# A new order for the first block of an attention and expert kernel

## The reference

```
def attention(x, y):                      # x: layernormed tokens, y: context
    q = (x @ Wq + bq).reshape(B, N, 16, 32)
    k = (y @ Wk + bk).reshape(B, M, 16, 32)
    v = (y @ Wv + bv).reshape(B, M, 16, 32)
    scores = einsum('bnhd,bmhd->bhnm', q, k) / sqrt(32)
    out = einsum('bhnm,bmhd->bnhd', softmax(scores), v).reshape(B, N, 512)
    return relu(out @ W1 + b1) @ W2 + b2
x = x + attention(layernorm(x), ctx)
top1 = argmax(x2n @ Wg.T)                 # one of 8 experts for each token
x = x + expert[top1](layernorm(x))        # 512 -> 128 (gelu) -> 512
```

## Time and profile before

| | us |
|---|---|
| median of 3 runs | 1470.18 (1470.04 to 1471.04) |
| the profiled execution | 1474.38 |
| its span, first to last instruction | 1472.6 |
| busy: PE, DVE, ACT, POOL | 1446.5, 1038.0, 756.6, 416.6 |
| granted clock of PE, mean of the span | 0.997 |

### The profile page before, as it was taken

The page is one execution under the profiler, slowest core; times in us unless marked ns, Lnnn a source line. Parts: engine busy times, 40 slices in busy tenths (PEclk is TensorE's granted clock), DMA queues, the critical chain, the costliest instruction groups (busy, mean ns, idle before and its releaser), DMA issues.

```text
span 1472.6 us, 23484 instructions
## 1 busy us (share of the span) xinstructions
PE 1446.5 (98%) x7710; PEld 1207.2 (82%) x7710; DVE 1038.0 (70%) x2524; ACT 756.6 (51%) x2097; POOL 416.6 (28%) x306
## 2 busy tenths in 40 slices
PE   7899999999999999999999999999999999999997
PEld 5688787878888888878787888888787878788996
DVE  5767667686868686776868686858676675748666
ACT  4656354544536353645455353635354544547875
POOL 1342221203122222222130312222222212108885
PEclk9999999999999999999999999999999999999999
DMA  7130201203030302131120301130202002357984
GB/s 284 45 102 1 87 1 44 66 27 105 22 100 1 108 15 94 38 84 47 43 81 22 101 13 67 43 90 1 86 1 66 22 29 87 140 176 249 300 262 147
DMA packets 70284, 121.50 MB, mean 83 GB/s; under 512 B 21847, under 2 KB 30304, under 8 KB 69142
## 3 DMA queue, kind: packets, MB, share of 16 engines
q1 hardware_dynamic: 59366, 86.30, 19.2%
q0 software_dynamic: 10800, 33.70, 6.0%
HBM read 75.09 MB, written 46.40 MB: 82 GB/s over the span
## 4 chain that ended last, share of the span: by engine, by line
PE 95%; DVE 3%; ACT 1%; issue 1%; DMA 0%; POOL 0%; POOLq 0%; SPq 0%; DVEq 0%; ACTq 0%
PE bank L1185 24%; PE bank L1207 24%; PE bank L1000 12%; PE bank L1137 8%; PE bank L1026 7%; PE bank L1607 4%; PE bank L1101 4%; PE bank L1645 3%; PE bank L1282 2%; PE bank L1591 2%; PE bank L968 2%; PE bank L1260 1%; DVE actH L1118 1%; ACT actH L1112 1%; PE bank L859 1%
## 5 line engine op out<-in xcount | busy, mean ns | idle before, releaser
L1207 PE MATMUL bank<-w,actH 128*128 128x512 f32 x1536 | 372.1, 393 | 0.0
L1185 PE MATMUL bank<-actA,w 128*128 128x512 f32 x1536 | 370.3, 394 | 0.0
L1185 PEld LDWEIGHTS bank<-actA,w 128*128 128x128 f32 x1536 | 284.2, 188 | 60.9
L1207 PEld LDWEIGHTS bank<-w,actH 128*128 128x128 f32 x1536 | 283.0, 188 | 55.9
L1095 POOL TENSOR_TENSOR E<-E,rc 128x1232 f32<-128x1232 f32 x64 | 144.2, 2254 | 461.3 <-DVE rc L1089 461.3
L1357 POOL DMA_INDIRECT region<-rows,pos x64 | 63.8, 997 | 456.4 <-DVE pos L1351 418.0
L1192 ACT ACTIVATE actH<-bank,b 128x512 fp32r<-128x512 f32 x128 | 88.5, 691 | 187.7 <-PE bank L1185 187.7
L1000 PE MATMUL bank<-actA,wq 128*128 128x512 f32 x768 | 182.4, 390 | 1.7 <-DVE actA L980 1.7
L1068 ACT ACTIVATE E<-bank,mx 128x77 f32<-128x77 f32 x512 | 157.7, 362 | 37.1 <-DVE mx L1035 37.1
L1000 PEld LDWEIGHTS bank<-actA,wq 128*128 128x128 f32 x768 | 144.1, 188 | 32.5 <-issue 2.7
L1014 DVE SCALAR_TENSOR_TENSOR actQ<-bank,bq,actQ 128x512 fp32r<-128x512 f32 x64 | 48.1, 751 | 167.9 <-ACT actQ L1009 167.9
(11 more groups left out here) (172 smaller groups left out, 2121.2 us busy)
## 6 DMA issues: line engine op xcount, KB each, us to landing
rowB<-region SPq DMA_DIRECT2D x71, 258.0 KB
xn<-in_x SPq DMA_DIRECT2D x64, 256.0 KB, 2.9
rows<-in_x SPq DMA_DIRECT2D x64, 256.0 KB, 3.4
w_raw<-in_W SPq DMA_DIRECT2D x2, 2048.0 KB, 11.8
e_raw<-in_E SPq DMA_DIRECT2D x16, 256.0 KB, 3.1
region<-padrow SPq DMA_DIRECT2D x9, 258.0 KB, 2.4
e_parts<-e_high SPq DMA_DIRECT2D x8, 256.0 KB, 2.0
e_parts<-e_low SPq DMA_DIRECT2D x8, 256.0 KB, 2.3
```

The costliest lines, as they stand in the source:

```text
L1185: mm = pe.matmul(p[:], w, a, start=k == 0 and j == 0, stop=k == KD - 1 and j == 2)
L1207: mm = pe.matmul(p[:], a, w, start=m == 0 and j == 0, stop=m == MF - 1 and j == 2)
```

## The change

The beginning of the program is put into another order, and the values are made in three pieces instead of four. The four batches' context rows are 4 x 77 = 308; before, each batch's 77 rows were a product (VP) of their own, now the 308 rows are cut into 128, 128 and 52. The steps that change place:

- KLO 0 and 1 (low parts of keys) stand behind the four XT, with KLO 2 and 3.
- W2's load is a step of its own behind the store of the keys.
- VP 0 stands ahead of the first queries, VP 1 between the scores of groups 1 and 2, VP 2 behind the scores of group 3; before, 2 and 3 stood among the probabilities' transposes and the first values products.
- The low part of a group of queries is a step of its own, QLO, no longer part of Q. In block 0 it stands further behind; in the later blocks directly behind its Q.
- The fourth queries and their QLO move among the scores of groups 0 and 1.
- MASKS moves ahead of the first queries, two W1 conversions move between the first three queries, and SUM of group 3 moves ahead of the first transposes.

```diff
+VR = [min(P, NB * M - i) for i in range(0, NB * M, P)]
+NV = len(VR)
...
-    v_parts = nc.dram_tensor("v_parts", [NB, M, 2, D], F32).ap()
+    v_parts = nc.dram_tensor("v_parts", [NB * M, 2, D], F32).ap()
...
             for c in range(NC):
                 step("PT", b, 0, c)
-            step("SUM", b, KD - 1)
+            if b:
+                step("SUM", b, KD - 1)
             for c in CA:
                 step("PT", b, 1, c)
             if b:
                 step("TT", b - 1, 0)
-            else:
-                step("VP", 2)
             step("AV", b, 0, "C")
             step("COPY", b, 0)
             step("AV", b, 0, "A")
             step("AV", b, 0, "B")
             if b:
                 step("TT", b - 1, 1)
-            else:
-                step("VP", 3)
...
-            if b == 0:
-                step("CONV_W1", 1)
...
         step("KP", 2)
-        step("KLO", 0)
-        step("KLO", 1)
         for s in range(SUB):
             step("XT", 0, s)
         step("KP", 3)
-        step("KLO", 2)
-        step("KLO", 3)
+        for m in range(KD):
+            step("KLO", m)
         step("KSTORE")
+        step("W2_LOAD")
         step("CONV_WQ", 1)
+        step("VP", 0)
         step("KCOPY")
+        step("MASKS")
+        step("VF", 0)
         step("Q", 0, 0)
-        step("Q", 0, 1)
-        step("VP", 0)
-        step("VF", 0)
+        step("QLO", 0, 0)
         step("VHI", 0)
-        step("Q", 0, 2)
         step("VLO", 0)
         step("VLOAD", 0, 0)
         step("VLOAD", 0, 1)
-        step("MASKS")
-        for g in range(KD):
-            for s in range(SUB):
-                step("S", 0, g, s)
-            if g == 0:
-                step("Q", 0, 3)
-            if g == 1:
-                step("VP", 1)
-            if g == 2:
-                step("VF", 1)
-            step("EXP", 0, g)
-            if g:
-                step("SUM", 0, g - 1)
-        step("VHI", 1)
+        step("VSTORE", 0)
         step("CONV_W1", 0)
-        step("VLO", 1)
-        step("VSTORE", 1)
+        step("Q", 0, 1)
+        step("QLO", 0, 1)
+        step("CONV_W1", 1)
+        step("Q", 0, 2)
+        for s in range(SUB - 1):
+            step("S", 0, 0, s)
+        step("QLO", 0, 2)
+        step("Q", 0, 3)
+        step("S", 0, 0, SUB - 1)
+        for s in range(SUB):
+            step("S", 0, 1, s)
+        step("QLO", 0, 3)
+        step("EXP", 0, 1)
+        step("SUM", 0, 0)
+        step("VP", 1)
+        for s in range(SUB):
+            step("S", 0, 2, s)
+        step("SUM", 0, 1)
+        for s in range(SUB):
+            step("S", 0, 3, s)
+        step("EXP", 0, 3)
+        step("VP", 2)
+        step("VF", 1)
+        step("SUM", 0, 2)
+        step("VF", 2)
+        step("SUM", 0, 3)
         step("XLOAD", 0)
...
-                mm = pe.matmul(p[0:M, :], ctxT[:, k, M * i:M * i + M], wv_raw[:, k, :],
+                mm = pe.matmul(p[0:VR[i], :], ctxT[:, k, P * i:P * i + VR[i]], wv_raw[:, k, :],
```

More of the change, by code:

```diff
@@ L166, in xattn_moe_kernel @@
     ctxT = staged("ctxT", [P, KT, NB * M])
-    v_f = [staged(f"v_f{i}", [M, D]) for i in range(2)]
-    bvbc = staged("bvbc", [M, D])
+    v_f = [staged(f"v_f{i}", [P, D]) for i in range(2)]
+    bvbc = staged("bvbc", [P, D])
     assert o[0] <= w2_at + size([P, MF, D], F32)
@@ L176, in xattn_moe_kernel @@
     w2_raw = at("w2_raw", [P, MF, D], F32, w2_at + 4 * MF * D)
[L177 to L180, removed]
+    assert NV == 3 and VR[0] >= M
+    v_hl = [at(f"v_hl{i}", [P, 2, D], F32R, (rows_at[1], xn_at)[i // 2] + i % 2 * size([P, 2, D], F32))
+            for i in range(NV)]
+    assert 2 * size([P, 2, D], F32) <= min(size([P, SUB, ROW], F32), SUB * size([P, D], F32))
     e1 = at("e1", [P, KD, NE, EH], F32, wq_at)
@@ L319, in attention_tail @@
             else:
-                for i in (2, 3):
-                    step("VF", i)
+                for i in (1, 2):
                     step("VHI", i)
-                for i in (2, 3):
+                for i in (1, 2):
                     step("VLO", i)
@@ L488, in xattn_moe_kernel @@
                 step("Y", b, 1)
-                step("Q", b + 1, 0)
-                step("Q", b + 1, 1)
+                for m in range(2):
+                    step("Q", b + 1, m)
+                    step("QLO", b + 1, m)
                 if prep is not None:
@@ L505, in xattn_moe_kernel @@
                         step("Q", b + 1, g + 2)
+                        step("QLO", b + 1, g + 2)
                 if b + 2 == NBLK:
@@ L607, in xattn_moe_kernel @@
         chains = []
-        DRIP = {"Q": 2, "PT": 2, "Y": 1, "TTOUT": 1}
+        DRIP = {"QLO": 2, "PT": 2, "Y": 1, "TTOUT": 1}
         def drip(n):
@@ L665, in sp_xnload @@
                 if b == 1:
-                    sp.wait_ge(st_v, 16 * (NB - 1))
+                    sp.wait_ge(st_v, 16 * NV)
                 if PREP0 + 2 <= b < PREP0 + 2 + NE:
@@ L702, in sp_vload @@
             else:
-                sp.wait_ge(st_v, 16 * (NB - 1))
+                sp.wait_ge(st_v, 16 * NV)
                 sp.wait_ge(S["pe_av"], 3 * NP * BPB * i)
             for c, r, k, m, h in PIECES[len(PIECES) // 2 * part:len(PIECES) // 2 * (part + 1)]:
-                src = v_parts[i, k:k + m] if i else f32(v_hl[0][k:k + m, :, :])
+                src = v_parts[M * i + k:M * i + k + m] if i else f32(v_hl[0][k:k + m, :, :])
                 src = src.rearrange("k s (g x) -> k (s g) x", g=NP)[:, :, HD * h:HD * h + HD]
@@ L716, in sp_vstore @@
             sp.wait_ge(S["dve_v"], i + 1)
-            sp.dma_start(v_parts[i], f32(v_hl[i][:])).then_inc(st_v, 16)
+            k = 0 if i else M
+            sp.dma_start(v_parts[P * i + k:P * i + VR[i]], f32(v_hl[i][k:VR[i]])).then_inc(st_v, 16)
         def sp_e1raw(sp, e):
@@ L866, in dve_vf @@
                 dve.wait_ge(S["pe_xT"], SUB)
-            dve.tensor_tensor(v_f[i % 2][:], of("VP", i)[0:M, :], bvbc[:], ALU.add).then_inc(S["dve_vf"], 1)
+            r = slice(0, VR[i])
+            dve.tensor_tensor(v_f[i % 2][r], of("VP", i)[r, :], bvbc[r], ALU.add).then_inc(S["dve_vf"], 1)
         def act_vhi(act, i):
             act.wait_ge(S["dve_vf"], i + 1)
-            act.activation(v_hl[i][:, 0], v_f[i % 2][:], ACT.Identity).then_inc(S["act_v"], 1)
+            r = slice(0, VR[i])
+            act.activation(v_hl[i][r, 0], v_f[i % 2][r], ACT.Identity).then_inc(S["act_v"], 1)
         def dve_vlo(dve, i):
             dve.wait_ge(S["act_v"], i + 1)
-            dve.tensor_tensor(v_hl[i][:, 1], v_f[i % 2][:], f32(v_hl[i][:, 0]),
+            r = slice(0, VR[i])
+            dve.tensor_tensor(v_hl[i][r, 1], v_f[i % 2][r], f32(v_hl[i][r, 0]),
                               ALU.subtract).then_inc(S["dve_v"], 1)
@@ L915, in pool_zero_row @@
         def pool_zero_row(pool):
-            pool.wait_ge(st_v, 16 * (NB - 1))
+            pool.wait_ge(st_v, 16 * NV)
             pool.wait_ge(ld_v, 16 * VLOADS)
@@ L1709, in xattn_moe_kernel @@
             "KSTORE": {"sp": sp_kstore},
+            "W2_LOAD": {"sp": sp_w2load},
             "CONV_WQ": {"act": act_conv_wq, "dve": dve_conv_wq},
@@ L1725, in xattn_moe_kernel @@
             "XNLOAD": {"sp": sp_xnload},
-            "Q": {"pe": pe_q, "act": act_q, "dve": dve_q},
+            "Q": {"pe": pe_q, "act": act_q},
+            "QLO": {"dve": dve_q},
             "S": {"pe": pe_s, "dve": dve_s, "act": act_s},
```

7 lines of the change are left out of this document (4 added, 3 removed).

## The result

The changed kernel takes 1460.69 us (median of four, 1460.08 to 1462.33) against 1470.61 us for the kernel before (four, 1470.04 to 1472.41). The ratio is 0.9932, with a 95% interval of 0.9915 to 0.9949: faster by 0.5 to 0.85%. The prediction was 1460.3 us in a range of 1456.8 to 1466.0. The profiled execution took 1462.33 us with a span of 1460.5, so the two profiled executions differ by 12.1 us while the medians differ by 9.9.

What follows compares the result with a forecast made beforehand. PE, busy 98%, bounds the kernel; time comes from its waits or work before H. One values product less (2.58), the gap (1.7) and remaining waiting and half-clock time make 9.9 off 1470.18: 1460.3 us, range 1456.8 to 1466.0.

Steps and rivals of the forecast that it cites:

- The walk: Step-by-step timing from the last key product to the first H product: H at 58.55 instead of 68.44 us, 9.9 gained.
- Rival B: PE's clock falls near 49 us, ahead of the values products, for about 6.8: gain 7.0, 1463.2 us; chance 30%.
- "Before, that low part, a values step and the masks held the first maximum", 3.8 gained: First softmax: third queries' low part queued behind three maxima, so exponentials start at 29.85 instead of 33.64 us, 3.8 gained.
- The fourth queries: Group 0's softmax: their copy on ACT, until 34.15 us, now ahead of tile 3's exponentials instead of behind; no separate gain given.
- VP(0) in the gap: First values product placed in PE's gap between last key product and first queries, 18.05 to 19.77 us: 1.7 us.
- One VP less: Values made on PE in three products instead of four: 2.58 us saved.
- SUM of group 3 ahead of the low parts: End of first softmax on DVE: group 3's sums at 45.8 to 47.2 us, low parts from 47.4; no price for the order.
- "Any difference behind H": Sign that the prediction is wrong: any difference after the first H product, where all engines' instructions read alike; no size.
- No stall for loads: First values product runs at 18.05 us without waiting for Wv, first products of values don't wait for gathers; loads cost nothing.

Runs made afterwards that it cites:

- before_fourth_queries: Kernel before with only the fourth queries ahead of group 0's last tile, their low part behind group 1's maxima: 1468.85 us, ratio 0.9984.
- values_behind_q1: Changed kernel with the first values product and its steps back behind the second queries: 1463.80 us, ratio 0.9954 to the kernel before.
- low_part_ahead: Changed kernel with the low part of the third queries back ahead of the first maxima: 1461.91 us, ratio 0.9940 to the kernel before.
- changed_again: Changed kernel run once more, unchanged, in a later group of runs: 1466.76 us, ratio 0.9935 to the kernel before.
- before_third_low_part: Kernel before with only the low part of the third queries moved behind the first three maxima: 1469.74 us, ratio 0.9987.
- the third group of runs: Runs of the changed kernel unchanged and two variants with the first softmax's end reordered; the kernel before took 1475.09 us there instead of 1470.61.

## Why the prediction was right, and where it was not

- **The walk.** It put H 42.22 us behind the last key product; the two profiles at the full clock, each one part away from the change, have 42.25 and 42.26, and after has 43.90 with its low clock. The intermediate stations agree within 0.1 us, counted from the key product: the end of Q(2) 12.58 predicted and 12.50 measured, the first exponential 13.52 and 13.53, EXP(1) 20.67 and 20.65, EXP(3) 28.12 and 28.10.
- **Which case.** Rival B, the fall of the clock, came by half. The clock fell near 49 us as priced, but was back after 3.41 us instead of 6.8, and cost some 1.65 instead of 2.9. The Trainium skill, "TensorE: Matmul & The Clock Gate", Part 1, says that the window over which activity is judged runs freely; by that, equal gaps may pass or fall, and the pair of 1.53 and 1.54 busy of 3.46 agrees with it. Whether every timed execution of the changed kernel falls cannot be told from the two profiles of it, both of which fell; three other kernels with the same two waits did not fall.
- **"Before, that low part, a values step and the masks held the first maximum", 3.8 gained.** This step's times came out, but not what it was said to bring. With the third low part put back, the first exponential came 0.94 us later and H at the same distance (42.26): in the changed kernel PE's own work sets the pace there, and that much of the earlier start is slack. Since ACT's wait ahead of EXP(1) still was 0.56 us, a delay by the whole 3.8 would have held up EXP(1); whether H would have come later by it is not shown.
- **The fourth queries.** The walk had them as one line among others ("before it stood behind it"). Alone on the kernel before they are worth 2.8 to 3.1 us at an equal clock (3.3 to 3.6 with it), as much as a whole values product: a copy queued behind the 5.02 us of exponentials on ACT held DVE, and PE behind it. (These are 16 exponentials; the x32 of the row, which the prediction read as 32, counts the 16 readings of their sums as well.)
- **VP(0) in the gap**, 1.7 predicted, measured 1.43. **One VP less**, 2.58 predicted, measured 2.94 where the fourth stood. The third stood in the tail as well, 2.58 us on the path in before_fourth_queries; now VP 2 stands beside group 3's softmax. I read that gain from the chains; no run moved it alone. Nor was the order of the keys' low parts, the masks, the W1 conversions or W2's load taken back alone.
- **SUM of group 3 ahead of the low parts.** The walk let it start the low parts at 47.4 and saw no price in it. It costs 0.75 us.
- **The parts and the whole.** At the full clock 1.43 + 2.94 + 2.84 + 2.58 - 0.75 is 9.0; from 51.64 (before at the full clock) to 42.25 is 9.4. Parts measured on two kernels need not add, and 2.58 is read from the chains. What is left over, 0.35, may be the keys' low parts behind XT: the queries' wait for the low parts of x was 1.72 us in before and is 1.19 in values_behind_q1. The low clock, 0.5 in before and 1.65 in after, takes 1.2 off the 9.4: the 8.2 between the two profiles.
- **"Any difference behind H".** By its own words the prediction would be wrong by one. The blocks behind H only shift with it (8.73 at H, 8.68 and 8.65 further on), but the expert stage differed by 3.4 us. Kernels with either order show that spread, so the sentence should have named it. The medians' 9.9 us is therefore no confirmation of the 9.9 of the walk to the tenth: the profiles show 8.7 at H (8.2 and 0.5 of an earlier start). That the median lies within 0.4 us of 1460.3 is in part luck.
- **No stall for loads.** VP(0) ran right behind the keys and the gathers held nothing: in PE's waits up to 100 us the only load is the first one, of Wk.

## What to carry to other kernels

Follow the chain until one engine has it without a gap: steps that free another engine inside that stretch are worth nothing as long as that engine's slack takes them up, and the same step may be worth 1.2 to 1.7 us in a kernel where that engine has the chain. A short copy queued behind a long run of exponentials on an engine that works in order can cost as much as a whole product (2.8 to 3.1 us here); look for what stands behind the long runs first. Price a low clock by what PE does in it, since slow products inside waits cost little and slow products on the path cost half their stretch.

## What was unexpected of the hardware

- The clock fell after two short waits (1.3 and 0.6 us) in two of two profiles of the changed kernel, and after the same waits not at all in low_part_ahead, values_behind_q1 and fourth_values_product.
- Low stretches at this place came as 3.41 us (after, changed_again, before_fourth_queries) and as 6.8 us (before, before_third_low_part), with the return in before_third_low_part after 5.92 busy of 6.83.
- The stage behind the last block's copy, the same work in all kernels, varied by 7.2 us between profiles (153.1 to 160.3), more than most parts of this change are worth. It was long in all three profiles of the third group of runs (158.8 to 160.3). The waits ahead of the experts' first product go with it (1.8 to 2.7 us in the four long ones, 0.3 in the others). What makes it vary stays open.
